# Window attention and routed experts on one core: a group's eight transposes in one block, one move, one block of values and denominators, and a new order

## The reference

```python
x = x + _L0_conv_ref(_ln_c(x), w_qkv, bias_table, w_proj, b_proj, rel_index)   # window attention
t = _to_tokens(x)
t = t + _L0_ffn_ref(_ln_t(t), router_w, router_b, expert_w, expert_b)          # top 2 of 8 experts
x = _from_tokens(t, x)
```

## Time and profile before

| | |
|---|---|
| median of 3 runs | 1163.12 us (1159.21 to 1164.28) |
| the profiled execution | 1159.65 us |
| its span, first to last instruction | 1157.9 us |
| mean granted TensorE clock | 0.982 of full speed |
| PE busy | 1047.0 us, 90% of the span |
| DVE busy | 867.9 us, 75% |
| ACT busy | 747.7 us, 65% |
| POOL busy | 476.4 us, 41% |

### The profile page before, as it was taken

The page is one execution under the profiler, slowest core; times in us unless marked ns, Lnnn a source line. Parts: engine busy times, 40 slices in busy tenths (PEclk is TensorE's granted clock), DMA queues, the critical chain, the costliest instruction groups (busy, mean ns, idle before and its releaser), DMA issues.

```text
span 1157.9 us, 39146 instructions
## 1 busy us (share of the span) xinstructions
PE 1047.0 (90%) x16838; PEld 596.0 (51%) x16838; DVE 867.9 (75%) x1345; ACT 747.7 (65%) x1217; POOL 476.4 (41%) x519
## 2 busy tenths in 40 slices
PE   4888899999999999999999999999999999998764
PEld 3455455555555555555555555555555545554321
DVE  4467788887877778787777787877787878678752
ACT  2587677776777666677777666777676667665400
POOL 1013434344344334543443344344433443445663
PEclk9999999999999999999999999999999999999976
DMA  5015567787877768787777687777776787646987
GB/s 188 2 39 131 117 162 175 181 199 188 184 177 163 170 151 196 183 191 180 167 179 173 158 193 188 181 179 166 180 177 164 190 192 174 174 105 148 205 188 192
DMA packets 49256, 192.49 MB, mean 166 GB/s; under 512 B 10558, under 2 KB 10814, under 8 KB 32572
## 3 DMA queue, kind: packets, MB, share of 16 engines
q1 hardware_dynamic: 49084, 189.98, 69.2%
HBM read 154.04 MB, written 18.87 MB: 149 GB/s over the span
## 4 chain that ended last, share of the span: by engine, by line
PE 56%; DVE 18%; DMA 9%; POOL 7%; issue 6%; ACT 2%; SPq 1%; POOLq 0%; ACTq 0%
PE bank L550 8%; PE bank L567 8%; PE bank L655 7%; DMA gz<-gates_dram 7%; PE bank L528 5%; PE bank L541 5%; DVE Ls L1746 4%; PE bank L584 4%; PE bank L591 3%; DVE probs L1687 3%; DVE mx L1680 3%; PE bank L603 3%; PE bank L498 3%; POOL vr L1483 2%; PE bank L612 2%
## 5 line engine op out<-in xcount | busy, mean ns | idle before, releaser
L655 PE MATMUL bank<-gz,wex 64*64 64x512 f32 x2048 | 261.9, 616 | 17.6 <-DVE gz L1702 13.2
L1492 POOL TENSOR_TENSOR gz<-gz,tt 128x1024 f32<-128x1024 f32 x96 | 237.7, 2477 | 55.7 <-DMA gz<-gates_dram 55.6
L1687 DVE TENSOR_TENSOR probs<-bank,mx 128x1024 f32<-128x1024 f32 x128 | 156.7, 1224 | 96.2 <-PE bank L567 93.2
L1077 ACT ACTIVATE pt<-bank 128x512 f32<-128x512 f32 x256 | 151.7, 592 | 115.9 <-PE bank L567 115.0
L1702 DVE TENSOR_TENSOR gz<-gz,tt 128x1024 f32<-128x1024 f32 x160 | 198.6, 1259 | 21.9 <-DMA gz<-gates_dram 21.9
L1453 POOL TENSOR_TENSOR tt<-prj,xs 128x512 f32<-128x512 f32 x64 | 82.4, 1309 | 290.6 <-ACT prj L1094 290.6
L1680 DVE TENSOR_REDUCE mx<-bank 128x16 f32<-128x1024 f32 x128 | 155.9, 1218 | 29.7 <-PE bank L550 28.8
L567 PE MATMUL bank<-cst,probs 128*128 128x128 f32 x1024 | 165.3, 284 | 2.9 <-ACT pt L1077 2.4
L567 PEld LDWEIGHTS bank<-cst,probs 128*128 128x128 f32 x1024 | 111.4, 141 | 87.6 <-issue 67.2
L550 PE MATMUL bank<-km,qs 32*64 32x128 f32 x4096 | 144.0, 276 | 2.9 <-issue 2.8
L655 PEld LDWEIGHTS bank<-gz,wex 64*64 64x64 f32 x2048 | 74.9, 136 | 135.6 <-issue 104.9
(11 more groups left out here) (110 smaller groups left out, 1436.2 us busy)
## 6 DMA issues: line engine op xcount, KB each, us to landing
gz<-gates_dram SPq DMA_DIRECT2D x256, 512.0 KB, 9.9
xs<-in_x SPq DMA_DIRECT2D x32, 512.0 KB, 9.1
tx<-tt SPq DMA_DIRECT2D x128, 128.0 KB, 2.8
out<-ob SPq DMA_DIRECT2D x128, 128.0 KB, 10.1
gz<-in_rel SPq DMA_DIRECT2D x1, 2048.0 KB, 8.1
gates_dram<-gt_rs SPq DMA_DIRECT2D x32, 64.0 KB
cst<-in_consts SPq DMA_DIRECT2D x1, 359.0 KB, 2.9
tt<-in_weights SPq DMA_DIRECT2D x4, 64.0 KB, 4.3
```

Of the source, the lines that this page charges most:

```text
L655: last = mm(bank[64 * x:64 * x + 64, Y_BANK + a, :], wex[64 * a:64 * a + 64, e, :], gz[64 * a:64 * a + 64, s.pair(e)[1], e % 2, x * CH:(x ...
L1077: af(pt[g % 2][:, u % 2, :, :, :, :].rearrange("p j h x q -> p (j h x q)"), bank[:, PT_BANK, :], ACT.Copy).then_inc(pt_ready, 1)
L1492: tt_(gz[:, k, e % 2, :], gz[:, k, e % 2, :], tt[s.buf(4)][:, :], op=ALU.mult).then_inc(z_pool, 1)
L1687: tt_(probs[g % 2][:, :, :, :].rearrange("p h w (m k) -> p (h w m) k", k=N), two_banks(S_BANK).rearrange("p (c k) -> p c k", k=N), mx[g % ...
```

## The change

`transposes`, `move_pt` and `values` now work on a whole group. The eight transposes of a group are one block: four into bank 4 and four into bank 5, which is also the bank of the group's values and denominators. The block waits for `o_ready` of the group before, because it writes over bank 5. One `move_pt` copies both banks, 128 x 1024. `values` holds the group's 16 products of values and then its denominators. The counts of the semaphores `t_full` and `pt_ready` go from 8 to 4 per strip.

```diff
-            def transposes(s, u):
-                g = u // 2
-                if u % 2 == 0:
-                    pe.wait_ge(exp_done, s.count(GROUPS, g + 1))
...
-                wait(pe, pt_ready, s.count(UNITS, u))
-                for j in range(2):
-                    for hp in range(2):
-                        at = 128 * (2 * j + hp)
-                        last = nc.tensor.transpose(bank[:, PT_BANK, at:at + 128],
-                                                   probs[g % 2][:, hp, 2 * (u % 2) + j, :], cv("ident"))
+            def transposes(s, g):
+                pe.wait_ge(exp_done, s.count(GROUPS, g + 1))
...
+                wait(pe, o_ready, s.count(GROUPS, g))
+                for u in range(2):
+                    for j in range(2):
+                        for hp in range(2):
+                            at = 128 * (2 * j + hp)
+                            last = nc.tensor.transpose(bank[:, PT_BANK + u, at:at + 128],
+                                                       probs[g % 2][:, hp, 2 * u + j, :], cv("ident"))
                 last.then_inc(t_full, 1)
...
-            def move_pt(s, u):
-                g = u // 2
-                act.wait_ge(t_full, s.count(UNITS, u + 1))
-                if u % 2 == 0:
-                    wait(act, od_full, s.count(GROUPS, g - 1))
-                af(pt[g % 2][:, u % 2, :, :, :, :].rearrange("p j h x q -> p (j h x q)"),
-                   bank[:, PT_BANK, :], ACT.Copy).then_inc(pt_ready, 1)
+            def move_pt(s, g):
+                act.wait_ge(t_full, s.count(GROUPS, g + 1))
+                wait(act, od_full, s.count(GROUPS, g - 1))
+                af(pt[g % 2][:, :, :, :, :, :].rearrange("p u j h x q -> p (u j h x q)"),
+                   two_banks(PT_BANK), ACT.Copy).then_inc(pt_ready, 1)
...
-                wait(dve, t_full, s.count(UNITS, 2 * g - 2))
+                wait(dve, t_full, s.count(GROUPS, g - 1))
```

More of the change, by code:

```diff
@@ L700, in _ @@
[L700 to L707 removed]
+            scores(strips[1], 1)
+            transposes(strips[1], 0)
+            project(strips[0])
+            values(strips[1], 0)
+            scores(strips[1], 2)
+            transposes(strips[1], 1)
@@ L770, in _ @@
-            value_rows(strips[3])
-            scores(strips[3], 3)
-            transposes(strips[3], 2)
-            project(strips[2])
-            queries(strips[4])
-            transposes(strips[3], 3)
-            channel_sums(strips[5])
-            values(strips[3], 0)
-            values(strips[3], 1)
-            router(strips[2])
-            denominators(strips[3], 0)
-            transposes(strips[3], 4)
-            transpose_logits(strips[2])
-            experts(strips[0], 0)
+            value_rows(strips[3])
@@ L784, in _ @@
+            values(strips[2], 3)
+            scores(strips[3], 2)
+            spread_std(strips[4])
+            transposes(strips[3], 0)
+            project(strips[2])
+            scores(strips[3], 3)
+            queries(strips[4])
+            values(strips[3], 0)
+            channel_sums(strips[5])
+            router(strips[2])
+            experts(strips[0], 0)
+            transpose_logits(strips[2])
+            transposes(strips[3], 1)
             keys(strips[4])
             experts(strips[0], 1)
+            values(strips[3], 1)
@@ L860, in _ @@
             experts(strips[-7], 7)
-            transposes(strips[-3], 2)
+            project(strips[-4])
+            transposes(strips[-3], 0)
             queries(strips[-2])
-            transposes(strips[-3], 3)
+            values(strips[-3], 0)
+            scores(strips[-3], 3)
+            transposes(strips[-3], 1)
+            channel_sums(strips[-1])
+            router(strips[-4])
             experts(strips[-6], 0)
+            experts(strips[-6], 1)
+            transpose_logits(strips[-4])
@@ L938, in _ @@
+            transposes(strips[-2], 3)
+            value_rows(strips[-1])
+            values(strips[-2], 3)
+            scores(strips[-1], 1)
+            transposes(strips[-1], 0)
             project(strips[-2])
-            experts(strips[-5], 7)
+            values(strips[-1], 0)
+            transpose_gates(strips[-3])
+            scores(strips[-1], 2)
             transposes(strips[-1], 1)
-            transpose_gates(strips[-3])
+            router(strips[-2])
+            transpose_logits(strips[-2])
@@ L1879, in _ @@
             top_two(strips[2])
+            normalise(strips[3], 1)
+            guard_variance(strips[5])
             row_max(strips[4], 0)
```

842 lines of the change are left out of this document (345 added, 497 removed).

## The result

The changed kernel takes 1228.6 us (median of 4 runs, 1224.6 to 1230.4) against 1163.7 before: ratio 1.055, with a 95% interval of 1.052 to 1.059 (below in the same form). Slower was right; the size was not: +65 us against the forecast +33, and 5.6 us above the range. The profiled execution took 1230.31 us.

The account below looks back on a forecast made before the run. TensorE, the fullest engine (1047 of 1157.9 us), was taken to bound the kernel. Per body 32.15 + 0.75 + 1.4 + 0.35 of pauses = 34.65 us against 33.23, x 25 = +35 us: 1196 us, range 1144 to 1223.

Parts of the forecast that it names:

- layout: New lists laid out by hand over one loop body: 32.15 us without DVE and POOL collisions, against 32.54 before.
- collisions: DVE operations with two SBUF inputs and POOL operations hold each other up: +0.75 and +1.4 us per body.
- Where the gates land: Gate DMAs behind the load: pair one at residual + 9.2 to 9.6 us, the fourth 25.2 us behind the residual.
- The second collision: POOL's gated(c-5,1) against top_two or guard_variance on DVE: +2.1 to +2.35 or +0.9 us, half the bodies each, +1.4.
- The router's part: POOL's gated(c-5,7) against DVE's gated delays the residual, and the router waits: +0.6 to +1.3 us, taken as +0.75.
- The pauses: TensorE pauses, 0.69 us per body, often fall where it would have waited anyway; half kept, 0.35 us.
- TensorE's own time: TensorE's busy time per loop body should stay within 0.3 us of 31.5 us.
- My 0.15 us saved by the merged blocks: Fewer changes of matrix form on TensorE: bounds 0 and -0.6 us per body, taken as -0.15.
- Start and end: Outside the steady bodies: start has spare engines, end is bound by gates coming back over DMA: 0 +- 8 us.
- collision in every body: Rival, 15%: pair one always lands inside top_two and the residual is late by 1.3 us: body 35.7, 1222 us.
- The collision-free rival: Rival, 22%: gates land outside top_two, the fourth pair early enough; -11 to -31 us, about 1142 us.

Follow-up runs that it names:

- experiment 5: Six already satisfied waits ahead of every experts block on TensorE: changed kernel 1232.6 us; changed kernel with the load behind two gate pairs 1164.7 us.
- the first edit of experiment 1: Changed kernel with POOL's gated(c-5,1) moved behind place_gates(c-4): 1227.0 us, ratio 1.056.
- Experiments 1 and 2: Changed kernel, single moves: gated(c-5,1) 1227.0 us, normalise 1232.2, gated of expert 7 1227.3; SP's load behind two gate pairs 1162.1, behind one 1164.5.
- the third edit of experiment 1: Changed kernel with POOL's gated of expert 7 put back behind the next body's residuals: 1227.3 us, ratio 1.057.

## Why the prediction was wrong

By its own terms, per body:

| | predicted | measured |
|---|---|---|
| TensorE busy | 31.3 | 32.50 |
| waits between blocks | 3.0 (0.85 layout, 0.75 and 1.4 collisions) | 1.71 (T 0.83, V 0.53, router 0.31, others 0.04) |
| pauses | 0.35 | 1.32 |
| sum | 34.65 | 35.59 (with 0.06 of small gaps) |

- *Where the gates land* was right: pair one at residual + 9.2 to 9.6 (measured 9.6), pair four at + 25.2 (25.8). *Collisions* were right in kind and number: ten bodies wait ahead of transposes(A,2) for 2.08 us on average, ten ahead of values for 1.32, twelve at the router. The second collision's two forms sum to 1.36 us against my 1.4. The router's part is 0.31 against 0.75, and the 0.85 us of waits that my layout had even without collisions are not there at all; that they are hidden in the longer body is likely, but was not tested.
- *The pauses* are the step that failed: "A pause on TensorE now often falls where it would have waited anyway; I keep half". The 0.69 us that I halved were only 0.38 of pauses to begin with, and these more than tripled, to 1.32 us a body. I had seen the pause and the DMA engines at 76% and did not put them together: the change bunched the data, the instruction packets came 6.5 us behind instead of 5.6 while it ran, and TensorE waited for 32 packets instead of 23 (experiment 5). A term that depends on the order of the transfers was carried over from the old order.
- *TensorE's own time* was the second: "TensorE's busy time in a body should stay within 0.3 us of 31.5" is missed: 32.50 us, 0.7 beyond that bound. The waits and pauses of 2 to 3 us, once they exist, drop the clock in eleven places, and each then costs more than its length. With the load behind one pair 23.3 us of busy time over 25 bodies are gone. My 0.15 us saved by the merged blocks looks right there, 31.57 us against 31.71 before, but isn't shown: with a quarter of the gates, where no pause disturbs, it is 31.51 (load behind two pairs) against 31.45.
- *Start and end*, 0 +- 8: measured +11.8, outside the bounds. The profiled execution lies 35 us above the forecast's 1195; about 24 of them are in the bodies and about 12 here. The versions with the changed start and end and all the gates have 8 to 16 us (10.9 with the load behind one pair: 174.0 and 163.7 us), so most of it is not the load's; what makes it was not looked into.
- *The rival "collision in every body"* had nearly the right time (1222, a body of 35.7) with the wrong reason, and that is luck: only ten bodies have the wait at the third transposes. *The collision-free rival* asked for gates outside `top_two` and an early fourth pair; the first edit of experiment 1 took `gated` out of `top_two` and gained nothing.
- The deeper fault is in how the sum was made: I priced SP's new order only through two instructions on POOL. Experiments 1 and 2 show that removing them one at a time gives nothing beyond the noise, and moving one `dma_start` group gives 64 us.

Open: why bodies of such different makeup all take 35.5 to 35.8 us. The changed kernel's chain of waits has one loop per body:

```profile
505.70 0.44 SPq L324
...
506.19 14.54 DMA gz<-gates_dram
520.73 0.07 issue
520.80 2.38 POOL gz L1356
...
524.73 2.39 POOL gz L1356
...
529.50 3.35 POOL tt L1317 x2
...
539.63 0.45 SPq L324
```

`experts(c-6,1)` frees a slot, the next pair is issued and takes 14.5 us among all the others, POOL's two last `gated` follow, the residual, and over the router the next body's `experts(c-6,1)`: 33.9 us here. The first pair ahead of the load, or a quarter of the data, shortens the transfer. But with the third edit of experiment 1 the chain is 54% TensorE, and the body is no shorter, so this loop alone doesn't explain it. Nor do the packets: in that version only 22 of 102 are waited for. That a pause is the wait for a packet, and that the gates' data delays the packets, is shown; how the 64 us split between pauses, waits behind late gates and the clock is only added up, not separated by a run.

## What to carry to other kernels

A wait put ahead of a group of DMAs is not priced by the first consumer that comes late: look whether the DMA engines stand idle while it lasts (2% busy for 8.4 us here, then 94%), since all the data then goes through in one bunch, and the instruction packets come late behind it. When a kernel gets slower by a rearrangement of many lists, try undoing the list of the DMA queue early; single collisions on the engines may be what the trace shows and yet give nothing back. And an idleness of 2 to 3 us on TensorE costs more than itself when the clock falls behind it.

## What the runs showed of the hardware that I had not expected

- TensorE pauses up to 3.2 us inside a block with no semaphore to wait for. All 137 such pauses over 0.3 us in these traces lie at a multiple of 256 of its instructions and end 1.2 to 1.8 us after a 16 KB instruction packet has landed. Pauses in 25 bodies: 0 in the three kernels with a quarter of the gates, 0.1 to 2.2 us where a gate DMA lands in 7.0 to 7.3 us (median), 9.5 to 52 where it takes 9.8 to 11.3; the exception is the old order with the load first (0.4 us at 10.9), whose TensorE waits 5.9 us in each body anyway.
- A single-input `tensor_scalar` of 0.28 us on DVE takes 2.39 us when it starts 0.1 us behind a POOL operation of 2.36 us: it waits out the whole of it. The 0.63 us of the earlier trace rows were already this: that operation started 0.49 us ahead of the other's end.
- One and the same wait of SP, the load's, costs 0 us behind the first pair and 64 us ahead of it.
